# Cross-attention block with a soft mixture of experts: the last attention tiles and the first slot tile in another order

## The reference

```
# block 1: cross-attention, 32 heads of 8, keys and values from ctx (32 x 64 x 128)
q = rope(layernorm(x) @ Wq);  k, v = split(ctx @ Wkv);  k = rope(k)
w = softmax(q k^T / sqrt(8));  x = x + (w v) @ Wout + bout
# block 2: soft mixture of 16 experts with 128 slots each, hidden width 64
x_ln   = layernorm(x) * gamma + beta
logits = l2norm(x_ln) * scale  @  l2norm(mu)          # per row: 16 experts x 128 slots
dispatch = softmax(logits over the experts)
combine  = softmax(logits over all 2048 slots)
slot_in  = dispatch^T x_ln                            # per sequence, expert, slot
h   = gelu(slot_in @ W1 + b1)
out = combine @ (h @ W2 + b2);   x = x + out
```

## Time and profile before

| | |
|---|---|
| median of three runs | 526.37 us (526.05 to 526.86) |
| the profiled execution | 526.87 us, of which the traced span is 525.0 us |
| PE busy | 471.5 us, 90% of the span |
| PE's weight loads | 378.8 us, 72% |
| DVE busy | 373.4 us, 71% |
| ACT busy | 300.5 us, 57% |
| POOL busy | 146.4 us, 28% |
| mean granted TensorE clock | 0.984 of full |

### The profile page before, as it was taken

The page is one execution under the profiler, slowest core; times in us unless marked ns, Lnnn a source line. Parts: engine busy times, 40 slices in busy tenths (PEclk is TensorE's granted clock), DMA queues, the critical chain, the costliest instruction groups (busy, mean ns, idle before and its releaser), DMA issues.

```text
span 525.0 us, 14893 instructions
## 1 busy us (share of the span) xinstructions
PE 471.5 (90%) x5776; PEld 378.8 (72%) x5776; DVE 373.4 (71%) x861; ACT 300.5 (57%) x595; POOL 146.4 (28%) x247
## 2 busy tenths in 40 slices
PE   0768899898888888969999999999999999999995
PEld 0545666666556564758888888888888888988884
DVE  5688989888889989475666575657657565755653
ACT  1345665556666555608447745854774585468454
POOL 3409511238393903211311211221121112112100
PEclk9969999999999999989999999999999999999999
DMA  6600000073001200000000000000000000000000
GB/s 184 227 7 6 7 7 6 8 165 90 7 10 36 32 0 2 2 1 1 12 11 2 12 11 0 10 10 10 0 10 10 7 3 10 10 0 10 11 12 10
DMA packets 16018, 12.75 MB, mean 24 GB/s; under 512 B 7232, under 2 KB 15344, under 8 KB 15600
## 3 DMA queue, kind: packets, MB, share of 16 engines
q1 hardware_dynamic: 15984, 12.27, 8.1%
HBM read 10.16 MB, written 2.11 MB: 23 GB/s over the span
## 4 chain that ended last, share of the span: by engine, by line
PE 60%; DVE 24%; ACT 8%; issue 5%; SPq 1%; DMA 1%; DVEq 1%; POOL 0%; ACTq 0%
PE psum L938 14%; PE psum L939 12%; PE psum L940 12%; PE psum L1149 9%; PE psum L1164 6%; DVE mx L689 5%; DVE rc L706 4%; DVE pb L694 3%; ACT vb L494 3%; PE psum L1017 2%; DVE pb L853 2%; DVE xT_l L658 2%; DVE ra L665 1%; DVE qkr L676 1%; ACT mu_raw L556 1%
## 5 line engine op out<-in xcount | busy, mean ns | idle before, releaser
L556 ACT COPY mu_raw<-psum 128x384 f32<-128x384 f32 x96 | 41.0, 445 | 116.4 <-PE psum L1149 116.4
L831 DVE TENSOR_REDUCE es<-eb 128x4 f32<-128x512 f32 x64 | 42.9, 686 | 61.2 <-ACT eb L548 61.1
L477 ACT ACTIVATE pb<-pb 128x512 f32<-128x512 f32 x64 | 39.3, 631 | 75.0 <-DVE pb L694 75.0
L1149 PE MATMUL psum<-w_raw,eb 64*128 64x129 f32 x1024 | 68.8, 286 | 3.0 <-DVE w_raw L824 1.9
L1149 PEld LDWEIGHTS psum<-w_raw,eb 64*128 64x128 f32 x1024 | 62.8, 193 | 8.2 <-DVE pb L853 4.0
L348 POOL TENSOR_TENSOR sm<-sm,mhalf 128x1 f32<-128x1 f32 x16 | 8.8, 551 | 169.9 <-DVE sm L810 169.9
L938 PE MATMUL psum<-mun_h,xlT_l 128*128 128x512 f32 x128 | 52.2, 408 | 0.2 <-DVE xlT_l L817 0.2
L1003 PE MATMUL psum<-ident,pb 128*128 128x128 f32 x256 | 42.2, 290 | 10.8 <-ACT vb L494 8.8
L853 DVE TENSOR_TENSOR pb<-psum,rh 128x384 f32<-128x384 f32 x96 | 49.3, 514 | 3.3
L1003 PEld LDWEIGHTS psum<-ident,pb 128*128 128x128 f32 x256 | 28.2, 145 | 31.5 <-issue 24.1
L940 PE MATMUL psum<-mun_h,xlT_h 128*128 128x512 f32 x128 | 50.6, 395 | 0.0
(11 more groups left out here) (156 smaller groups left out, 1076.6 us busy)
## 6 DMA issues: line engine op xcount, KB each, us to landing
mu_raw<-in_L_ffn_mu SPq DMA_DIRECT2D x1, 2048.0 KB, 12.9
out<-w_raw SPq DMA_DIRECT2D x16, 128.0 KB, 1.7
xa<-in_x SPq DMA_DIRECT2D x1, 1536.0 KB, 8.5
ctile<-in_ctx SPq DMA_DIRECT2D x16, 64.0 KB, 1.8
eb<-mur_scratch SPq DMA_DIRECT2D x1, 1024.0 KB, 4.9
w_raw<-in_L_ffn_W SPq DMA_DIRECT2D x2, 512.0 KB, 7.9
w_raw<-in_L_ffn_W SPq DMA_DIRECT2D x1, 1024.0 KB, 9.3
xa<-in_x SPq DMA_DIRECT2D x1, 512.0 KB, 3.5
```

The costliest lines, as they stand in the source:

```text
L556: a.copy(eT[:, e0:e0 + n, :].rearrange("p n (b k) -> p b n k", b=2), pair(i, n)[:, :, :, HC:XC]).then_inc(eT_ready, 1)
L831: v.reduce_sum(es[:, 4 * c:4 * c + 4], eb[:, 4 * c:4 * c + 4, :], AX.X).then_inc(es_ready, 1)
L1149: m = mm(bank[HB[i % 3] + b][:, n * XC:(n + 1) * XC], eb[rows, e, :], xw[rows, e, :], start=True, stop=True)
```

## The change

Only orders are changed. No operation is added and none removed, and no shape changes. Three helpers get an argument that says which of the four chunks they treat.

- PE: `slot_logits(0)` is cut in three. Chunks 0 and 1 stay where they were. Chunk 2 follows the last transposes of attention tile 15, and chunk 3 follows `project_out` of tile 14. Behind `attend` of tile 15 and `expand(0)`, `transpose_xl(1, 1)` now stands ahead of `project_out` of tile 15. Two waits of PE go: for `x1_ready` ahead of `expand(0)`, and for `e_ready` ahead of the last `project_out`.
- ACT: `sumsq(1, 1)` moves ahead of the exponentials of tile 0, which are cut in two halves around the last two copies of the transposed numerators.
- DVE: `clamp(0, 0)` moves ahead of `xlT_copy(0)`. The set-up of `b2s` and two of the four `slot_sums(0)` move ahead of `residual` of tile 14, the other two behind it. `normalise` of tile 15 follows at once; `xw_copy(0)` and `xlT_copy(1)` now stand ahead of `residual` of tile 15, and `sums(0, 0)` behind it.

```diff
--- before.py
+++ after.py
@@ -540,10 +540,10 @@
                 act.wait_ge(xl_ready, t + 1)
                 a.activation(sq, xl[:, p, :], ACT.Square, accum_out=ss[:, p:p + 1]).then_inc(ss_ready, 1)
 
-            def slot_exps(t, p):
+            def slot_exps(t, p, chunks=range(4)):
                 act.wait_ge(rn_ready, t + 1)
                 wait(act, es_ready, t * 4)
-                for c in range(4):
+                for c in chunks:
                     act.wait_ge(l_filled, t * 4 + c + 1)
                     a.activation(eb[:, 4 * c:4 * c + 4, :].rearrange("p a b -> p (a b)"), bank[LB[c]][:], ACT.Exp,
                                  scale=rn[:, p:p + 1], bias=nshift[:]).then_inc(e_ready, 1)
@@ -581,10 +581,11 @@
             sumsq(0, 0)
             for gr in range(2):
                 pT_copy(TILES - 1, gr)
-            slot_exps(0, 0)
+            sumsq(1, 1)
+            slot_exps(0, 0, range(2))
             for gr in range(2, 4):
                 pT_copy(TILES - 1, gr)
-            sumsq(1, 1)
+            slot_exps(0, 0, range(2, 4))
             with act.Fori(0, TILES // 2 - 1) as i:
                 for p in range(2):
                     ffn_step(i * 2 + p, p)
@@ -824,9 +825,9 @@
                     v.tensor_tensor(xw[:, 8 * c:8 * c + 8, 0:HID], bank[2 + c].rearrange("p (e h) -> p e h", h=HID),
                                     b1b[:, 8 * c:8 * c + 8, :], ALU.add).then_inc(xw_ready, 1)
 
-            def slot_sums(t):
-
-                for c in range(4):
+            def slot_sums(t, chunks=range(4)):
+
+                for c in chunks:
                     dve.wait_ge(e_ready, t * 4 + c + 1)
                     v.reduce_sum(es[:, 4 * c:4 * c + 4], eb[:, 4 * c:4 * c + 4, :], AX.X).then_inc(es_ready, 1)
 
@@ -896,26 +897,27 @@
             softmax(TILES - 1, 1, 0)
             softmax(TILES - 1, 1, 2)
             residual(TILES - 3)
+            clamp(0, 0)
             xlT_copy(0)
-            clamp(0, 0)
             normalise(TILES - 2)
-            residual(TILES - 2)
             dve.wait_ge(wb_loaded, 96)
             v.memset(b2s[:].bitcast(F32), 0.0).then_inc(b2_step, 1)
             v.memset(es3[:].bitcast(F32).rearrange("p a e -> p (a e)"), 0.0).then_inc(es_zeroed, 1)
             dve.wait_ge(b2_step, 1)
             v.tensor_copy(b2s[0:3 * EXPERTS, :], b2_raw[:]).then_inc(b2_step, 1)
             dve.wait_ge(b2_step, 2)
-            dve.wait_ge(es_zeroed, 1)
             v.tensor_tensor(b2s[2 * EXPERTS:3 * EXPERTS, :], b2_raw[2 * EXPERTS:3 * EXPERTS, :],
                             b2s[2 * EXPERTS:3 * EXPERTS, :].bitcast(F32), ALU.subtract).then_inc(b2_ready, 1)
+            slot_sums(0, range(2))
+            residual(TILES - 2)
+            slot_sums(0, range(2, 4))
+            normalise(TILES - 1)
             dve.wait_ge(xw_const, 3)
-            slot_sums(0)
-            sums(0, 0)
-            normalise(TILES - 1)
-            residual(TILES - 1)
             xw_copy(0)
             xlT_copy(1)
+            residual(TILES - 1)
+            dve.wait_ge(es_zeroed, 1)
+            sums(0, 0)
             ffn_step(0, 0)
             dve.wait_ge(st2_ready, TILES)
             moments(st2, ln2, TILES - 4, TILES, 1 + LN_EPS, LN_EPS * LN_EPS, var_step, 7, var_ready)
@@ -1108,9 +1110,9 @@
                     m = nc.tensor.transpose(bank[1][:, k * P:(k + 1) * P], xl[:, p, k * P:(k + 1) * P], ident[:])
                 m.then_inc(xlT_filled, 1)
 
-            def slot_logits(t):
+            def slot_logits(t, chunks=range(4)):
                 pe.wait_ge(xlT_ready, t + 1)
-                for c in range(4):
+                for c in chunks:
 
 
                     if c == 2:
@@ -1193,20 +1195,20 @@
             for gr in range(2):
                 transpose_p(TILES - 1, 1, gr, more=False)
             pe.wait_ge(mu_ready, 2)
-            slot_logits(0)
+            slot_logits(0, range(2))
             for gr in range(2, 4):
                 transpose_p(TILES - 1, 1, gr, more=False)
+            slot_logits(0, range(2, 3))
             for k in range(KD):
                 project_out(TILES - 2, k)
+            slot_logits(0, range(3, 4))
             attend(TILES - 1, 1, roped=False)
-            pe.wait_ge(x1_ready, TILES - 1)
             pe.wait_ge(w12_ready, 2)
             expand(0)
+            transpose_xl(1, 1)
             pe.wait_ge(b2_ready, 1)
-            pe.wait_ge(e_ready, 4)
             for k in range(KD):
                 project_out(TILES - 1, k)
-            transpose_xl(1, 1)
             ffn_step(0, 0, first=True)
             ffn_step(1, 1)
             with pe.Fori(1, TILES // 2 - 1) as i:
```

## The result

The changed kernel takes 521.88 us as the median of seven runs (519.52 to 523.02), the kernel before, in the same series, 526.86 us (526.05 to 530.59). The ratio is 0.9875, with a 95% interval of 0.9837 to 0.9913: faster, by 1.25%. A second series gave 520.83 us for 527.48 and a ratio of 0.9859 (0.9828 to 0.9889).

A forecast was written before the change was run, and what follows sets the result against it. From tile 1's first logits on, PE's own work was taken to bound the kernel; 4.4 us ahead of `dispatch(0)` and 1.85 in it make 6.25, taking 526.37 to 520.1 us, range 519.2 to 522.1.

The forecast's parts named there:

- The point on which all hangs: Start of tile 1's slot logits on PE: 233.45 instead of 239.69; the end comes earlier by the same amount.
- The two gaps: PE's waits ahead of `dispatch(0)`, 2.34 us for `oT` of tile 15 and 1.95 us for `xw_copy`: both go.
- The clock's share: Gain inside `dispatch(0)`: 1.85 of the 6.25 us, if the clock stays at 1.00.
- Switches of PE between streams: Two added returns to a matmul stream ahead of `attend` of tile 15: 0.1 us each, bounds 0 and 0.3.
- The new wait in dispatch: Fourth group of `dispatch(0)` waits for the first `hidden` result: 0.6 us, released at 231.65.
- at full clock a group takes 0.65: Twelve matmuls of `dispatch(0)` at full clock, from 48 taking 5.17 us at half clock: 0.65 us.
- The covered edits: Earlier `clamp(0, 0)` on DVE and `sumsq(1, 1)` ahead of ACT's exponentials: covered by slack, cost nothing.
- The rule on the clock's window: TensorE's clock falls by activity in a freely running window, so a fall could differ between executions; no size given.
- the likeliest case: Whole kernel with the forecast gain of 6.25 us: 520.1 us, own range 519.3 to 521.0, chance 0.78.
- the clock's fall in `dispatch(0)`: Rival: `dispatch(0)` still takes 6.3 us, only the 4.4 us ahead of it are won: 522.0 us, chance 0.08.
- DVE as the bound: Rival: DVE runs without pause from `attend` to `hidden`; a 1 us slip leaves 5.25 us gain: 521.1 us, chance 0.10.
- the 0.4 us by which a median moves: Whole-kernel time: allowance for scatter of the median in the likeliest case's range, 0.4 us.

The follow-up runs named there:

- the filled kernel: Kernel before plus thrown-away matmuls on PE, 9 ahead of the last `project_out` and 8 behind `transpose_xl(1)`: stretch from logits to logits 22.38 us, ratio 0.9946.
- the second execution: The changed kernel run and profiled again with no edit: stretch from logits to logits 17.80 us, span 518.4 us, median of six runs 520.83 us.
- The one with the last tile filled: Changed kernel plus thrown-away matmuls in the last tile, 6 ahead of the transpose of the sums and 5 ahead of `combine`: 520.40 us, ratio 0.9831.

## Why the prediction was right, and where it was not

- **The point on which all hangs**, the start of tile 1's logits: forecast 233.45, found 233.13. The gain of the stage is 6.72 us for 6.25.
- **The two gaps are DVE's order.** Shown: DVE's list alone wins 6.06 us, and putting one `residual` back costs 2.3.
- **The clock's share**, forecast at 1.85 us: 1.93 us by the filled kernel (`dispatch(0)` 4.33 us for 6.26). The granted clock is 1.00 throughout the stretch in both profiles of the changed kernel.
- **Switches of PE between streams** were put at +0.2 us and gave -0.17: from the first logit to `attend` it is 7.50 us for 7.67. This is two misses that cancel. The 24 passes of the logits in three pieces take 6.04 us (2.86, 1.49 and 1.69) for 5.68, so the cuts cost 0.36 and not 0.2. But `project_out` of tile 14 is followed by the next stream after 0.67 us (220.48 to 221.15), and by `attend` before after 1.11 (221.74 to 222.85), and the transposes give back another 0.09. What a switch costs depends on what meets what; the forecast was taken from one such place.
- **The new wait in dispatch** was put at 0.6 us and is 0.23. The step that failed is "at full clock a group takes 0.65": I halved the time at half clock. A group takes 0.73 us at full clock, so these matmuls don't follow the clock in full, and DVE is nearer to keeping pace than I thought. The step had no part in the forecast start of the logits, which was chained on `hidden`: from `hidden` to the logits it takes 2.64 us (230.49 to 233.13), as forecast. The 0.3 us by which the logits came early are those by which `hidden` did (230.49 for 230.8), and 0.2 of them come from `attend` (222.84 for 223.05).
- **The mean clock** was to rise from 0.984 to about 0.99. The profile has 0.983, since the fall in the last tile replaced the one removed; the second execution, without it, has 0.990.
- **The covered edits** cost and give nothing (17.81 us without them), and nobody waits for ACT's delayed exponentials.
- **The total** was 520.1 us; the median is 521.88, in the range, but above the 521.0 of the likeliest case. That it lies inside is partly luck: the range was stretched to 522.1 for two rivals (the clock's fall in `dispatch(0)`, DVE as the bound), and neither happened. The term that was mis-sized is "the 0.4 us by which a median moves": three runs within 0.81 us had stood for the scatter, and the claim that 0.2% can be told from no change rests on the same. Seven runs of before reach from 526.05 to 530.59, and the medians of the two kernels lie 4.98 us apart in the first series and 6.65 in the second. The profiles show one place where it comes from: the last tile, at 16.0 or 18.0 us in the changed kernel and at 16.1 or 18.2 in the one before. The early part may be a second (first slot logit at 215.18 to 217.11 over all profiles), but that isn't shown, as the two programs that were profiled twice gave it within 0.04 us each.
- **The rule on the clock's window.** The trace of before couldn't tell whether a fall differs between executions. The runs show both. In the transition it came in both profiles of the kernel before (`dispatch(0)` 6.26 and 6.46 us). In the last tile the same program gives 2.08 or 3.38 us (changed kernel), and 2.09 or 3.68 (before). The Trainium skill's freely running window ("TensorE: Matmul & The Clock Gate", Part 1, the HAM clock gate) agrees with the second. No run shows the window itself. Three equal times had stood as evidence for a fall in every execution. They were no evidence, as the seven runs show; that the fall came in both profiles of the transition bears the conclusion out for these two and leaves the other executions open.

What stays open: what decides in an execution whether the clock falls in the last tile, and what delays the first logit by up to 1.9 us. The last store took 3.35 us in one profile and 2.27 to 2.36 in the others; no run here tells why. Starting `hidden` ahead of ACT's copy of the same group was not tried.

No version clearly beats the changed kernel. The one with the last tile filled has the lowest ratio, with an interval that overlaps.

## What to carry to other kernels

Where two passes of a kernel meet, look at each in-order list for an instruction that PE waits for and that stands behind work nobody waits for yet. Here the new order of VectorE's list alone was worth 6.1 of 6.7 us, and the elaborate interleaving of the matmuls, on top of it, 0.7. A gap on TensorE is to be priced with what the clock does behind it. And before a wait in a loop is filled, take the engine's own work time from rows at the same clock, or the wait looks larger than it is, and look up what the work behind the moved piece waits for.

## What the hardware showed that I had not expected

- 12 matmuls of 64x129 from a 64x128 weight take 1.29 us at clock 0.50 and 0.73 us at 1.00, a factor of 1.76. A pass of 128x512 takes 0.233 us at 1.00.
- Two PE gaps of 2.3 and 2.0 us with 1.3 us of work between them brought the clock down in both profiles of the kernel before, and gaps of 0.72 and 2.17 us with 1.1 us between them did so in one profile. One gap of 2.22 us behind dense work did not, in one profile.
- In the last tile, one program shows the clock down or up in its `combine` from execution to execution, behind the same two waits: 3.38 or 2.08 us (changed kernel), 3.68 or 2.09 (before).
